# A graph attention layer: each piece of 256 edges gathered once into a ring and copied to its walk entries by SyncE's DMAs, edge features transposed by the host's layout

## What is computed

```python
h   = relu(layernorm(x))
xm  = h @ W_n2m.T                       # N x 128
ea  = edge_attr_32 @ W_r2m.T            # E x 128
# a loop edge is added for each node, with the mean of its edges' features
xl  = xm @ Wl.T + bl;  xr = xm @ Wr.T + br      # 8 heads of 16
u   = leaky_relu(xl[src] + xr[dst] + ea @ We.T, 0.2)
logits = sum over a head of u * att             # E x 8
alpha  = softmax of logits over the edges of one dst
out = segment_sum(xl[src] * alpha, dst) + bias
return x + out @ W_m2n.T
```

## Time and profile before

| | |
|---|---|
| time, median of 3 runs | 3654.3 us (3628.19 to 3661.28) |
| span of the profiled execution, first to last instruction | 2427.2 us |
| the profiled execution's own time | not given with its profile |
| mean granted TensorE clock | 0.984 |
| first gather of the loop, last gather | 127.7 us, 2285.0 us |
| busy, share of the span | PE 93%, DVE 61%, ACT 59%, POOL 71% |
| DMA engines | 101 GB/s on average |

### The profile page before, as it was taken

One profiled execution on the slowest core, in us unless ns is written; L12 is line 12 of the kernel. 1 busy time (PEld: TensorE's weight loads), 2 busy tenths in 40 slices (PEclk: granted clock), 3 DMA queues, 4 the chain that ended last, 5 costly groups with the idle time before them and its releaser, 6 DMA issues. The chain is left out here.

```text
span 2427.2 us, 71208 instructions
## 1 busy us (share of the span) xinstructions
PE 2249.0 (93%) x16556; PEld 1730.1 (71%) x16557; DVE 1481.8 (61%) x4178; ACT 1438.7 (59%) x4332; POOL 1722.3 (71%) x1914
## 2 busy tenths in 40 slices
PE   3968999989999999999999999999999999999977
PEld 2745777767777777777777777777777777777756
DVE  4734656656666666566656665666566656666677
ACT  2714666656665666566656665666566656666653
POOL 3777777777777777777777777777777777777501
PEclk9989999999999999999999999999999999999999
DMA  6244444444444444444444444444444444444117
GB/s 199 80 110 94 103 103 98 97 101 105 99 100 101 106 98 98 101 107 98 98 101 106 98 99 102 106 99 99 101 105 98 99 102 106 98 99 99 47 45 130
DMA packets 288536, 244.85 MB, mean 101 GB/s; under 512 B 168519, under 2 KB 259624, under 8 KB 287842
## 3 DMA queue, kind: packets, MB, share of 16 engines
q1 hardware_dynamic: 221742, 116.00, 21.3%
q0 software_dynamic: 60704, 120.20, 21.2%
q10 hardware_dynamic: 5652, 3.68, 0.5%
HBM read 228.23 MB, written 19.40 MB: 102 GB/s over the span
## 5 line engine op out<-in xcount | busy, mean ns | idle before, releaser
L778 POOL DMA_INDIRECT xl_g<-xl_table,src_tab x1708 | 1637.8, 959 | 522.9 <-issue 515.0
L999 DVE SCALAR_TENSOR_TENSOR uT<-banks,relu 128x256 f32<-128x256 f32 x854 | 347.3, 422 | 544.4 <-issue 517.8
L860 PE MATMUL banks<-msg,onehot 128*128 128x177 f32 x3416 | 632.3, 328 | 7.0 <-DVE acc L955 2.6
L860 PEld LDWEIGHTS banks<-msg,onehot 128*128 128x128 f32 x3416 | 516.8, 191 | 168.8 <-issue 152.3
L898 ACT ACTIVATE distance<-iota_n,minus_slot 128x128 f32<-128x128 f32 x1708 | 541.1, 390 | 0.0
L813 PE MATMUL banks<-ident,xl_g 128*128 128x128 f32 x3416 | 464.2, 280 | 36.2 <-DMA xl_g<-xl_table,src_tab 35.8
L813 PEld LDWEIGHTS banks<-ident,xl_g 128*128 128x128 f32 x3416 | 443.5, 201 | 44.5 <-DMA xl_g<-xl_table,src_tab 43.8
L913 ACT ACTIVATE relu<-banks 128x256 f32<-128x256 f32 x854 | 315.9, 383 | 149.6 <-PE banks L813 116.0
L794 PE MATMUL banks<-onehotT,xr_parts 128*128 128x256 bf16 x2562 | 356.4, 276 | 23.8 <-issue 18.6
L903 ACT ACTIVATE onehot<-distance 128x512 f32<-128x512 f32 x427 | 269.0, 630 | 113.9 <-PE banks L860 101.4
L907 ACT ACTIVATE rbfT<-banks 128x128 f32<-128x128 f32 x427 | 116.5, 273 | 353.5 <-PE banks L808 342.1
(11 more groups left out here) (200 smaller groups left out, 1642.2 us busy)
## 6 DMA issues: line engine op xcount, KB each, us to landing
slot_bc<-slot_dram SPq DMA_DIRECT2D x427, 128.0 KB
xl_g<-xl_table,src_tab POOLq DMA_INDIRECT x1708
rbf<-in_edge_attr SPq DMA_DIRECT2D x854, 32.0 KB
masks<-masks_dram SPq DMA_DIRECT2D x864, 12.1 KB
out<-in_x SPq DMA_DIRECT2D x16, 336.0 KB
out<-result POOLq DMA_DIRECT2D x6, 896.0 KB, 9.5
xl_table<-lr_sb SPq DMA_DIRECT2D x49, 64.0 KB, 1.5
xl_in<-xl_table SPq DMA_DIRECT2D x7, 448.0 KB, 4.7
```

Source lines behind the costliest of these rows:

```text
L778: pool.indirect_dma_start(out=xl_g[:, k % RING, t], out_offset=None, in_=xl_table, in_offset=bass.IndirectOffsetOnAxis(ap=src_tab[:, e:e + ...
L860: mm = nc.tensor.matmul(U_ps[h], onehot[:, j % 2, t], msg[:, j % 2, t], start=i == 0, stop=i == PT - 1)
L999: nc.vector.scalar_tensor_tensor(out=uT[:, s % 2, h * PIECE:(h + 1) * PIECE], in0=z_ps[h], scalar=SLOPE, in1=relu[:, h], op0=ALU.mult, op1 ...
```

## The change

1. GpSimd gathers each piece once, two indirect DMAs a piece, 1612 in all, into `xl_p`, a ring of 16 pieces. Each gather waits for the landing of the one eight before it (`FLIGHT`), and every four pieces for z of the entries that used the buffers (`free_tab`). Each gather also raises `landed` by one when the engine is done with it.
2. SyncE copies a piece from `xl_p` to its place in `xl_g` for each walk entry, two DMAs a step, when `landed` shows that eight more gathers were issued after the piece's.
3. The host gives the edge features twice: as rows by piece (`attr_rows`, loaded into `rbf` 13 steps late, ring of 8) and transposed by piece (`attr_cols`, loaded into `attrT`, ring of 4). The transpose on TensorE and its copy on ACT go; the edge term is one matmul of 256 columns for each half.
4. The masks of a batch of eight steps come with two DMAs instead of sixteen; `slot_bc` gets a ring of 4, the masks of 2. SyncE's turn reads four table entries (two pieces for now, two for the late load).
5. The host lays out dst by pieces and the sources as columns, so `meta_dram`, `src_rows` and the transposes of `src_tab` leave the prologue.

```diff
-SRING = 8
-MRING = 3
+SRING = 4
+TRING = 4
+ARING = 8
+PRING = 16
+FREED = 4
+MRING = 2
+LATE = LAG - 4
+GATHERS = PT * PIECES
+FLIGHT = 8
...
         @block.sync
         def _(sp):
-            for k, s, r in sweep(sp, 0, 4 * BATCH, STEPS, MASK_ROWS, UNROLL, UNROLL):
-                if inside(k, STEPS):
-                    if inside(k - RING, STEPS):
-                        sp.wait_ge(attr_ready, TICK * (k - RING + 1))
-                    for h, e in enumerate(entries(nc, mybir.EngineType.SP, edge_tab, k, E - PIECE)):
-                        sp.dma_start(rbf[:, s % RING, h * PT * D_RBF:(h + 1) * PT * D_RBF],
-                                     edge_attr[bass.DynSlice(e, PIECE), :].rearrange("(p i) k -> p (i k)", i=PT)
-                                     ).then_inc(loads[s % RING], 16)
-                    if inside(k - SRING, STEPS):
-                        sp.wait_ge(ohT_ready, k - SRING + 1)
-                    sp.dma_start(slot_bc[:, s % SRING], slot_dram[one(k)].broadcast_to([P, GROUP])
-                                 ).then_inc(slots_in[s % SRING], 16)
+            for k, s, r in sweep(sp, -2, 4 * BATCH, STEPS - 2, STEPS + LATE, UNROLL, UNROLL):
+                b = None if (s - BATCH // 2) % BATCH else r * (UNROLL // BATCH) + s // BATCH
+                if has(b):
+                    at_m = s // BATCH % MRING
+                    if inside(b - MRING, BATCHES):
+                        sp.wait_ge(last_ready, b - MRING + 1)
+                    for h in range(SPLIT):
+                        of = batch_masks[one(b), :, h].rearrange("a k m -> (a k) m").unsqueeze(1)
+                        sp.dma_start(masks[h * ROWS:(h + 1) * ROWS, at_m], of.broadcast_to([BATCH, HEADS, MASKS])
+                                     ).then_inc(masks_in[at_m], 16)
...
+                if inside(k + 2, STEPS):
+                    q = (s + 2) % SRING
+                    if inside(k + 2 - SRING, STEPS):
+                        sp.wait_ge(ohT_ready, k + 2 - SRING + 1)
+                    sp.dma_start(slot_bc[:, q], slot_dram[one(k + 2)].broadcast_to([P, GROUP])
+                                 ).then_inc(slots_in[q], 16)
+                if inside(k, STEPS + LATE):
+                    pieces = entries(nc, mybir.EngineType.SP, piece_tab, k, PIECES - 1, 2 * SPLIT)
+                    now, late = pieces[0:SPLIT], pieces[SPLIT:]
+                if inside(k, STEPS):
+                    if inside(k - TRING, STEPS):
+                        sp.wait_ge(z_done, Z * (k - TRING + 1))
+                    for h in range(SPLIT):
+                        sp.dma_start(attrT[h * D_RBF:(h + 1) * D_RBF, s % TRING],
+                                     attr_cols[one(now[h])].rearrange("a k e -> (a k) e")
+                                     ).then_inc(turned_in[s % TRING], 16)
+                if inside(k - LATE, STEPS):
+                    n = (s - LATE) % ARING
+                    if inside(k - LATE - ARING, STEPS):
+                        sp.wait_ge(attr_ready, TICK * (k - LATE - ARING + 1))
+                    for h in range(SPLIT):
+                        sp.dma_start(rbf[:, n, h * PT * D_RBF:(h + 1) * PT * D_RBF],
+                                     attr_rows[one(late[h])].rearrange("a p k -> (a p) k")
+                                     ).then_inc(loads[n], 16)
+                if inside(k, STEPS):
+                    if inside(k - RING, STEPS):
+                        sp.wait_ge(msg_ready, TICK * (k - RING + 1))
+                    sp.wait_ge(landed, now[SPLIT - 1] * PT + (PT + FLIGHT))
+                    sp.sem_inc(landed_seen, 1)
+                    for h in range(SPLIT):
+                        sp.dma_start(xl_g[:, s % RING, h * PT:(h + 1) * PT],
+                                     xl_p[:, one(now[h] & (PRING - 1))].rearrange("p a i d -> p (a i) d")
+                                     ).then_inc(xl_in[s % RING], 16)
...
         @block.gpsimd
         def _(pool):
-            for k in range(STEPS):
-                if k >= RING:
-                    pool.wait_ge(msg_ready, TICK * (k - RING + 1))
-                for t in range(TILES):
-                    e = TILES * k + t
-                    pool.indirect_dma_start(out=xl_g[:, k % RING, t], out_offset=None, in_=xl_table,
-                                            in_offset=bass.IndirectOffsetOnAxis(ap=src_tab[:, e:e + 1], axis=0)
-                                            ).then_inc(gathers[k % RING], 16)
+            for j in range(GATHERS):
+                g, i = divmod(j, PT)
+                if j % (PT * PRING) == 0 and g >= PRING:
+                    freed = entries(nc, mybir.EngineType.Pool, free_tab, (g - PRING) // PRING, Z * (STEPS + 1), PRING // FREED)
+                if j % (PT * FREED) == 0 and g >= PRING:
+                    pool.wait_ge(z_done, freed[g % PRING // FREED])
+                    pool.sem_inc(free_seen, 1)
+                if j >= FLIGHT:
+                    pool.wait_ge(landings[j % FLIGHT], 16 * (j // FLIGHT))
+                pool.indirect_dma_start(out=xl_p[:, g % PRING, i], out_offset=None, in_=xl_table,
+                                        in_offset=bass.IndirectOffsetOnAxis(ap=src_tab[:, j:j + 1], axis=0),
+                                        engine_sem=landed).then_inc(landings[j % FLIGHT], 16)
...
         @block.tensor
-                    pe.wait_ge(rbfT_ready, k + 1)
-                    for i in range(PT):
-                        for h in range(SPLIT):
-                            q = slice(h * PT * D_RBF, (h + 1) * PT * D_RBF)
-                            nc.tensor.matmul(z_ps[h][:, i::PT], Wc2[q, i], rbfT[q, n], start=False, stop=False)
-                if inside(k + 1, STEPS):
...
-                    nc.tensor.transpose(rbfT_ps, rbf[:, n], ident[:]).then_inc(rbfT_done, 1)
-                if inside(k, STEPS):
-                    pe.wait_ge(gathers[s % RING], (r * (UNROLL // RING) + s // RING + 1) * GATHERED)
+                    pe.wait_ge(turned_in[s % TRING], (r * (UNROLL // TRING) + s // TRING + 1) * FULL)
+                    for h in range(SPLIT):
+                        q = slice(h * D_RBF, (h + 1) * D_RBF)
+                        nc.tensor.matmul(z_ps[h], Wc[q], attrT[q, s % TRING], start=False, stop=False)
+                    pe.wait_ge(xl_in[s % RING], (r * (UNROLL // RING) + s // RING + 1) * FULL)
```

More of the change, by code:

```diff
@@ L81, in one, with entries @@
     return slice(k, k + 1) if isinstance(k, int) else bass.DynSlice(k, 1)
-def entries(nc, engine, tab, k, top):
-    at_k = slice(SPLIT * k, SPLIT * k + SPLIT) if isinstance(k, int) else bass.DynSlice(SPLIT * k, SPLIT)
+def entries(nc, engine, tab, k, top, width=SPLIT):
+    at_k = slice(width * k, width * k + width) if isinstance(k, int) else bass.DynSlice(width * k, width)
     _, values = nc.values_load_multi_w_load_instructions(
         tab[0:1, at_k], engines=[engine], min_val=0, max_val=top,
-        skip_runtime_bounds_check_because="the prologue counts the walk's windows and edges within these bounds")
+        skip_runtime_bounds_check_because="the prologue counts the walk's windows and pieces within these bounds")
     return values
@@ L159, in gat_kernel, with prologue @@
         finale(nc, banks, x, xl_table, xr_parts, ident, ident16, att_bc, Wc, W_outT, bias_col, acc, out)
-def prologue(nc, banks, xl_table, meta_dram, slot_dram, masks_dram, inputs,
-             xr_parts, ident, ident16, ones, iota_n, node_of, att_bc, att_pad, Wc, Wc2, W_outT,
-             bias_col, minus_slot, src_tab, win_tab, edge_tab):
-    x, src, dst, W_n2m, W_r2m, Wl, bl, Wr, br, We, att, bias, W_m2n = inputs
+def prologue(nc, banks, xl_table, slot_dram, masks_dram, inputs,
+             xr_parts, ident, ident16, ones, iota_n, node_of, att_bc, att_pad, Wc, W_outT,
+             bias_col, minus_slot, src_tab, win_tab, piece_tab, free_tab):
+    x, src_cols, dst_rows, dst_lasts, W_n2m, W_r2m, Wl, bl, Wr, br, We, att, bias, W_m2n = inputs
@@ L484, in _ @@
             mm.then_inc(walk_spread, 1)
+            pe.wait_ge(met_ready, 1)
+            nc.tensor.matmul(free_ps, ones[0:WINDOWS, 0:1], met[:], start=True, stop=True).then_inc(met_counted, 1)
             pe.wait_ge(wT_ready, 2)
@@ L1368 @@
     nc = bacc.Bacc("TRN2", target_bir_lowering=False, num_devices=1)
+    given = laid_out(inputs)
+    plain = {n: inputs[n] for n in _PLAIN}
     arrays, args = {}, []
-    for name in _INS:
-        a = np.ascontiguousarray(inputs[name])
+    for name, a in [("x", plain.pop("x")), *given.items(), *plain.items()]:
+        a = np.ascontiguousarray(a)
         arrays[f"in_{name}"] = a
```

213 lines of the change are left out of this document (103 added, 110 removed).

## The result

The changed kernel takes 3934.2 us (3932.89 to 3934.92, 4 runs) against 3653.8 us (3628.19 to 3661.28, 4 runs) of the kernel before: a ratio of 1.0787, with a 95% interval of 1.0749 to 1.0825. It is slower by 280 us, where 202 had been forecast. (Ratios are given here with their intervals as they are on record; the quotient of two medians can differ a little, here it is 1.0767.) The sign is the forecast's; the profile shows that its reason is not.

A forecast was written before the change was run, and what follows sets the result against it. GpSimd's gathers bound the kernel before; SyncE would bound the changed one: 115.2 + 15.4 + 215 + 384 x 5.58 (2142.7) + 3 + 138.3 = 2629.6 us, 202.4 over 2427.2, so 3654.3 + 202.4 = 3857 us; range 3550 to 3940.

The forecast's parts named there:

- those 1227 us: Median run time of the kernel before (3654.3 us) above its profiled span (2427.2); unexplained by the trace, carried over unchanged.
- SyncE's step: SyncE's work per loop step after the change: 5.08 + 0.40 + 0.10 = 5.58 us, setting the pace; chance 0.55.
- rivals 3: Timed runs have TensorE at half its clock, so PE is the bound: 213 us less, 3440 us; chance 0.11.
- Rival 4: Time around the span goes on the inputs, which grow with edge features given twice: over 4000 us; chance 0.04.
- the table load: SyncE's load of four table entries instead of two, each step: 0.10 us more, with 0 to 0.65 possible.
- Stalls: Delays of SyncE's DMAs within a step: 0.42 us today for five DMAs, kept at 0.40 for seven.
- the trace disagrees: Claim that starting DMAs is not small here: 0.357 us of queue time per 32 KB, 3.88 us a step, engines 44% busy.
- POOL waiting for z_done: Sign that the forecast is right: gaps between GpSimd's gathers, with POOL waiting for z; no size given.
- a gain of 4%: GpSimd's part: 1612 gathers at 1.281 us instead of 1708, 2065 us, 92 less.
- L808 and rbfT: TensorE's transpose and ACT's copy go: PE saves 0.2 to 0.3 us a step, priced at nothing as beside the bound.
- Rival 1: GpSimd stays the bound if SyncE's step is under 4.84 us: 102 us less, 3552 us; chance 0.20.
- the 0.984: TensorE's granted clock over the whole span of the earlier trace, held against TensorE running at half its clock.

## Why the prediction was right or wrong, point by point

**The base: wrong, and the step that failed.** "Nothing in the trace tells what those 1227 us are; I carry them over unchanged." The step that failed is the one from the sum to the time: 202 us for SyncE's step, laid on 3654.3. The sum was made at a level the timed runs were not at. At their level the 280 us are not SyncE's step: PE waits 8.4 us for the copy, and a DMA less on SyncE gives 9. They come with the bursts that the wait for z makes, which the sum has at nothing: 3439 with bursts of four, 3934 with eight. The span of 3653.2 in the repeat of before shows that those us lie within the steps, where a change of the steps can move them. Two numbers of one kernel that stand 50% apart say that the trace is of something else than the times, and no sum from that trace is worth its decimals. My chances for the ways in which the two could differ (rivals 3 and 4) named neither waits held by another engine's issue nor the price of bursts. That the time still came out slower, at the upper end of 3550 to 3940, is luck.

**The sum at its own level: right.** 2629.6 us of span were predicted and 2644.8 measured there, 215 us over before where I had 202. First gather 115.1 us (predicted 115.2): the wait for meta_dram went, and the projection of the earlier trace rows starts at 50.57 where it started at 62.16, as the changed kernel's row shows. First copy 130.2 (predicted 130.6).

```profile
50.57 1.09 ACT L436 ACTIVATE minus_rows<-x_sb,shift,rstd 128x256 f32<-128x256 f32 x2 [0.78 <-DVE shift L610]
```

From the first copy to the last 2372.7 (predicted 43 x 5.0 + 384 x 5.58 = 2357.7). From the last copy to z 7.2 instead of 3, from there to the end 134.7 instead of 138.3. The order of the bounds is shown too: moving one DMA off SyncE gave 239 us. The DMA engines were busy 55% of the time, less than the 69% estimated.

**Within the step, errors cancelled.** Free of stalls I had 5.08 + 0.10 for the table load; it is 4.99. The load of four entries takes 0.398 us at the median, less than the 0.646 of two before, and not the 0.75 I named: the load, from another table, was cheaper, so 0.25 less than before and not 0.10 more, 0.35 below my term. Against this, the copy of xl_g holds SyncE's queue for 0.507 us and not for the 0.357 of an rbf DMA from which I had priced it, 0.15 each, 0.30 a step. That makes 0.05 of the 0.19 by which the free step is shorter; the rest I haven't traced. Stalls took 0.58 (5.57 less 4.99) where 0.40 was left.

The Trainium skill (Runtime: NRT & Kernel Launch, Instruction fetch mechanics) puts a register load at about 200 ns a register, which would make 0.8 us for four. It states this for loads from HBM, and the tables here lie in SBUF, so as a figure for this load it was stretched. The 0.398 measured does not bear it out here, nor the extrapolation from two that I used.

The Trainium skill (DMA: Bandwidth & Descriptors, Issuing engines are not separate DMA queues) holds the time to start DMAs for usually small beside the DMA. Here 0.507 us of SyncE a copy, seven DMAs a step, set the pace at 2430, with the DMA engines at 55%. No row here times the landing of these DMAs, so whether the start is small beside them stays open; what the runs show is that it can be the bound, and the prediction's "the trace disagrees" was more than its rows said.

**GpSimd: counted right, weighed wrong.** 1612 gathers, 1.25 us apart inside a burst, where 1.28 was predicted. But of the new waits the prediction weighed only that for a landing. The one "every four pieces for z" stands in it as a sign to look for ("POOL waiting for z_done"), with no price and no reason for having none. It made bursts of eight: parted at 1.7 us, 191 of 207 groups of gathers in the changed kernel. At 2430 the kernel before has a steady stream; at 3640 it has bursts too, 166 of four and 118 of eight among 289. At 3640 that is the price of the change: with FREED = 2 it is 197 us faster than before, with 4 it is 280 slower. The prediction had all of part 1 of the change as a gain of 4%.

**How 3934 comes out.** In the rows above with FREED = 4, eight gathers take 9.7 us (1500.70 to 1509.43 and 0.94), then GpSimd waits 8.4: 18.1 us a burst, which times 1612/8 = 201.5 is 3647, and with the 257 us of both ends 3904, within 1% of the time. This adds up what was measured and does not yet explain the wait. The burst of the result's trace does: of its wait of 7.64 us, 2.02 pass until ACT starts, 1.04 until PE starts, and 4.6 are PE's work at the lower clock, 2.08 more than at the full one. Ahead of 203 bursts that work took 4.62 us at the median, and in 172 of them its last matmul ran at the slower pace. An estimate from these rows: 172 x 2.08 = some 360 us of the 3934. In the kernel before at 3640 the z matmul takes 275 ns at the median, in the changed one 377.

**PE, ACT and the rivals.** L808 and rbfT went as said. At 2430, with SyncE as the bound, that was beside it; what it is worth at 3640 was not tested. Rival 1 (GpSimd stays the bound) is nearly what is seen once slot_bc leaves SyncE: its first and last gather stand at 114.2 and 2249.5 us, 1.325 us apart on average where it had 1.281, and even that was no faster than before by more than the measurement tells. Rival 3 had a grain of truth: the clock is lower in the timed runs (0.78 to 0.84), but behind PE's idle stretches and not in place of them. In before with the 1 us break it is 0.90 at both levels (0.901 and 0.897), so the level as such doesn't lower it. It isn't free, though, since PE's work behind a burst is what GpSimd waits for. And the 0.984 that I set against this rival says less than I took it for: in the stretch of the earlier trace rows the granted clock reads 1.00 while the pitch of the transposes halves, so there the slow pace does not show in it. Rival 4 falls: the time is inside the span.

**What is shown and what is not.** Shown: at 3640 the length of a burst of gathers and the break after it change the time (3934 to 3439 by one number; 3636, 3301, 3115 by the break in before; 3925 to 3470 by it in the changed kernel). SyncE's load does not with bursts of eight (9 us), but does with bursts of four (149 us). Read off the traces, but not tested by itself: that it is ACT's wake-up from TensorE's semaphores and SyncE's instructions that are held while gathers are issued, and what the lower clock behind a burst costs. Open: what in the chip holds them, why only at one of two levels, how much of the 496 us of FREED = 2 is the clock, and whether a break of 1 us brings the changed kernel to its 3097 us there. A gather's own duration, 0.94 us, is the same at both levels, and so doesn't tell them apart.

## What to carry to other kernels

Before a trace is used for a sum, hold its execution's own time against the timed runs; where they part, the first experiment is the old kernel again. A ring whose buffers come free in large lots turns a steady stream of GpSimd gathers into bursts, and a burst can stop engines that have nothing to do with it: free buffers in small lots, or tie the gathers to the steps of the work (tested here on the kernel before alone), and time it where the slow level shows. An engine that is left idle by this can start again at the lower clock, and the same work then takes longer (4.62 us for 2.54 here), just where others wait for it. And a DMA cost SyncE 0.33 to 0.51 us at the median, so count an engine's issues like its instructions before giving it copies.

## What the runs showed of the hardware that was not expected

- One kernel, two times: 2429 and 3640 us, with all runs of a set at one level, and one chip number on record at both.
- While GpSimd issues indirect DMAs 1.25 us apart, at the 3640 level ACT started 7.7 us after the matmul it waits for had ended, in the burst shown. SyncE's pairs of DMAs for rbf and xl_g, which start 1.27 us apart in a free step (1506.84 to 1508.11 in the trace at 2430), started 4.43 us apart there, with the DMA engines at 38%.
- A write of 1024 columns on GpSimd that serves nothing took 521 us off the kernel there (3636 to 3115), and added 683 at the other level (2429 to 3112).
- After PE had stood idle from 2012.69 to 2017.97 the granted clock read 0.50, and L825 to L834 took 4.62 us instead of 2.54.
- Loading four entries of `tabs` into registers on SyncE took 0.398 us at the median, loading two of `edge_tab` in the kernel before 0.646.
